# Sums of the next step's first group moved between W1 and W2 products at a step's end, on one Trainium2 core

## What is computed

```python
def step(h, _):
    agg = jax.ops.segment_sum(h[src], dst, num_segments=N) / deg
    diff = jnp.tanh(jax.nn.gelu(agg @ W1 + b1, approximate=False) @ W2 + b2)
    h = h + (diff - decay * h) * dt
    return (h, None)
...
h = jnp.maximum(_layernorm(x, axis=-1), 0.0)
x = x + _L0_gnn_ref(h, edge_index, ...)      # twelve steps
h = jnp.maximum(_layernorm(x, axis=-1), 0.0)
x = x + _L1_gnn_ref(h, edge_index, ...)      # two graph convolutions
```

## Time and profile before

| what | value |
|---|---|
| time, median of 3 runs | 1358.31 us (1358.14 to 1360.56) |
| the profiled execution: its own time | 1362.37 us |
| its span, first to last instruction | 1360.7 us |
| TensorE busy | 1276.2 us, 94% |
| VectorE busy | 392.7 us, 29% |
| ScalarE busy | 323.7 us, 24% |
| mean granted TensorE clock | 0.981 of full |

### The profile page before, as it was taken

How to read it: one execution, slowest core, us unless ns; L and a number is a source line. 1 busy time by engine, 2 the same in 40 slices (tenths; PEclk the granted TensorE clock), 3 DMA queues, 4 the chain that set the end, 5 groups by cost and what they waited for, 6 DMA issues and landing times.

```text
span 1360.7 us, 17338 instructions
## 1 busy us (share of the span) xinstructions
PE 1276.2 (94%) x7201; PEld 712.6 (52%) x7201; DVE 392.7 (29%) x792; ACT 323.7 (24%) x474; POOL 45.2 (3%) x48
## 2 busy tenths in 40 slices
PE   2875999999999999999999999999999999979998
PEld 1764356455564555545545556455554554545545
DVE  6899013113121131221311312113112131451312
ACT  1788113113121131221311312113112121330100
POOL 3900000000000000000000000000000000000000
PEclk7899999999999999999999999999999999979999
DMA  3000200000000000000000000000000001120101
GB/s 95 1 1 0 61 1 0 0 0 0 0 0 0 0 0 0 0 0 0 0 0 0 0 0 0 0 0 0 0 0 0 0 0 39 47 57 0 47 17 33
DMA packets 24541, 13.66 MB, mean 10 GB/s; under 512 B 6171, under 2 KB 23605, under 8 KB 24384
## 3 DMA queue, kind: packets, MB, share of 16 engines
q1 hardware_dynamic: 22414, 12.28, 3.5%
q10 hardware_dynamic: 1698, 0.66, 0.2%
q0 software_dynamic: 400, 0.33, 0.1%
HBM read 9.42 MB, written 3.44 MB: 9 GB/s over the span
## 4 chain that ended last, share of the span: by engine, by line
PE 86%; DVE 7%; issue 3%; ACT 2%; DMA 2%; DVEq 0%; ACTq 0%; SPq 0%; POOL 0%; POOLq 0%
PE ps L630 34%; PE ps L632 32%; PE ps L653 10%; PE ps L644 8%; DVE scratch L996 4%; ACT scratch L787 1%; PE ps L557 1%; PE ps L680 1%; DVE ps L1102 1%; DMA adj<-packed_scratch,adj 1%; ACT adj L755 1%; DMA dinv_scratch<-cols 1%; DVE lo L979 0%; DMA adj<-adj 0%; PE ps L520 0%
## 5 line engine op out<-in xcount | busy, mean ns | idle before, releaser
L630 PE MATMUL ps<-adj,hi 128*128 128x512 f16 (+2 forms) x2450 | 814.5, 353 | 9.3 <-DVE lo L979 5.8
L632 PE MATMUL ps<-adj,lo 128*128 128x512 f16 (+2 forms) x2352 | 796.2, 353 | 0.0
L630 PEld LDWEIGHTS ps<-adj,hi 128*128 128x128 f16 x2450 | 238.3, 97 | 260.2 <-issue 21.8
L632 PEld LDWEIGHTS ps<-adj,lo 128*128 128x128 f16 x2352 | 229.3, 98 | 242.9 <-issue 23.0
L1102 DVE TENSOR_TENSOR ps<-ps,bias 128x512 f32<-128x512 f32 (+1 forms) x84 | 53.8, 641 | 538.0 <-PE ps L653 538.0
L795 ACT ACTIVATE scratch<-ps 128x512 f32<-128x512 f32 (+1 forms) x84 | 46.3, 551 | 644.8 <-DVE ps L1102 644.8
L644 PE MATMUL ps<-scratch,w 128*128 128x512 f32 (+2 forms) x336 | 141.5, 544 | 18.3 <-ACT scratch L787 18.3
L787 ACT ACTIVATE scratch<-ps,b1c,cols 128x512 f32<-128x512 f32 (+2 forms) x168 | 113.4, 722 | 159.7 <-PE ps L644 158.9
L653 PEld LDWEIGHTS ps<-w,scratch 128*128 128x128 f32 x1200 | 145.0, 194 | 6.3
L653 PE MATMUL ps<-w,scratch 128*128 128x128 f32 x1200 | 147.7, 277 | 0.0
L1095 DVE TENSOR_TENSOR scratch<-ps,scratch 128x512 f32<-128x512 f32 (+2 forms) x84 | 52.0, 619 | 187.6 <-PE ps L644 132.2
(11 more groups left out here) (129 smaller groups left out, 210.1 us busy)
## 6 DMA issues: line engine op xcount, KB each, us to landing
scratch<-rdeg_scratch SPq DMA_DIRECT2D x1, 1562.5 KB
state<-in_x_dram SPq DMA_DIRECT2D x5, 256.0 KB, 4.1
scratch<-in_x_dram SPq DMA_DIRECT2D x5, 256.0 KB, 2.8
x_scratch<-state SPq DMA_DIRECT2D x5, 256.0 KB, 2.8
scratch<-dinv_scratch SPq DMA_DIRECT2D x5, 256.0 KB, 3.8
state<-x_scratch SPq DMA_DIRECT2D x5, 256.0 KB, 4.1
out_dram<-state SPq DMA_DIRECT2D x5, 256.0 KB
adj<-adj SPq DMA_DIRECT2D x1, 390.6 KB, 4.0
```

Source lines behind the costliest of these rows:

```text
L630: nc.tensor.matmul(bank, hi[:, k, :], adj[:, k, c0:c0 + n], start=(at == 0), stop=False)
L632: mm = nc.tensor.matmul(bank, lo[:, k, :], adj[:, k, c0:c0 + n], start=False, stop=(k == K_ORDER[-1][0]))
```

## The change

`edge_sums` gets a range of source tiles, and the sums of group 0 are taken in two parts. The first part (`HEAD`, eight source tiles, groups 0 and 1; in the last step `LAST_HEAD`, four tiles) is issued at the end of the step before, between `hidden(TAIL)` and `outputs(5)`. Within it the four `hi` products of source group 0 come first and then the four `lo` products. `hidden(TAIL)` writes to a bank of its own (`ps_hid_tail`, both halves in bank 7), so it no longer waits for `gelu(5)`. ScalarE and VectorE are reordered at a step's end: four `next_hi` now stand ahead of `tanh(4)` and `gelu(5)`, `next_lo(0)` ahead of `add_bias(4)`, `next_lo(1)` to `next_lo(4)` ahead of `add_bias(5)`. In the last step `norm_rows` goes from ScalarE to VectorE, as one `tensor_scalar` for each tile without the ReLU (which `norm_hi` and `lo_of` now do), `row_factors` is cut at tiles 12 and 20 and not at 12 and 16, and its parts move.

```diff
+HEAD = 2 * GROUP_TILES
+LAST_HEAD = GROUP_TILES
...
+        ps_hid_tail = [ps[:, 7, 0:P], ps[:, 7, P:2 * P]]
...
-            def edge_sums(turn, g, split, first):
+            def edge_sums(turn, g, split, first, part=(0, TILES)):
...
-                for at, (k, owner) in enumerate(K_ORDER):
+                for at in range(*part):
+                    k, owner = K_ORDER[at]
+                    if g == 0 and owner == 0:
+                        if at == 0:
+                            pe.wait_ge(his, first + 1)
+                            for i in range(GROUP_TILES):
+                                product(hi, K_ORDER[i][0], i == 0, False)
+                            pe.wait_ge(los, first + 1)
+                            for i in range(GROUP_TILES):
+                                mm = product(lo, K_ORDER[i][0], False, False)
+                        continue
...
                 def hidden(g):
...
-                    pe.wait_ge(s_gelu, t * 2 * NG + 2 * g + OPEN)
+                    pe.wait_ge(s_gelu, t * 2 * NG + (2 * g if g < TAIL else 0) + OPEN)
...
                 hidden(TAIL)
+                pe.wait_ge(s_aggT, t * NG + TAIL - 1 + OPEN)
+                if last:
+                    pe.wait_ge(s_diag, 1)
+                    edge_sums(STEPS, 0, (c_hi[0], c_lo[0]), 0, (0, LAST_HEAD))
+                else:
+                    edge_sums(t + 1, 0, (s_hi, s_lo), (t + 1) * NG, (0, HEAD))
                 outputs(TAIL - 1)
                 outputs(TAIL)
+            edge_sums(0, 0, (s_hi, s_lo), 0, (0, HEAD))
...
# VectorE, steps 1 to 11
                 means(TAIL)
+                dve.wait_ge(s_now, t + 1)
+                next_lo(0)
                 add_bias(TAIL - 2)
+                next_lo(1)
                 update(TAIL - 2)
-                dve.wait_ge(s_now, t + 1)
-                for g in range(3):
+                for g in range(2, 5):
                     next_lo(g)
                 add_bias(TAIL - 1)
                 update(TAIL - 1)
-                for g in range(3, TAIL - 1):
-                    next_lo(g)
...
# VectorE, last step
+            def norm_rows(g):
+                k0, nt = GROUPS[g]
+                dve.wait_ge(s_fac, 1 if g < 3 else 2 if g < 5 else 3)
+                dve.wait_ge(s_x2o[g], 16 * parts(g))
+                for k in range(k0, k0 + nt):
+                    last_ = V.tensor_scalar(state[:, k, :], state[:, k, :], ln_a[:, k:k + 1], ln_b[:, k:k + 1],
+                                            ALU.mult, ALU.add)
+                last_.then_inc(s_t, 1)
...
                     if g == 4:
                         row_factors(0, 12)
-                    if g == 5:
-                        row_factors(12, 16)
+                        for b in range(3):
+                            norm_rows(b)
                 means(TAIL)
-                add_loops(TAIL)
+                norm_lo(0)
                 add_bias(TAIL - 2)
+                norm_lo(1)
                 update(TAIL - 2)
-                norm_lo(0)
                 add_input(TAIL - 2)
+                row_factors(12, 20)
+                norm_rows(3)
                 add_bias(TAIL - 1)
+                norm_lo(2)
+                norm_rows(4)
                 update(TAIL - 1)
-                norm_lo(1)
-                norm_lo(2)
+                norm_lo(3)
                 add_input(TAIL - 1)
+                norm_lo(4)
                 add_bias(TAIL)
                 update(TAIL)
                 add_input(TAIL)
-                row_factors(16, TILES)
-                for g in range(3, NG):
-                    norm_lo(g)
+                row_factors(20, TILES)
+                norm_rows(5)
+                norm_rows(6)
+                add_loops(TAIL)
+                norm_lo(5)
+                norm_lo(6)
```

More of the change, by code:

```diff
@@ L611, in _, with product @@
                 pe.wait_ge(g_degk, 5 + OPEN)
-            def edge_sums(turn, g, split, first):
+            def edge_sums(turn, g, split, first, part=(0, TILES)):
                 c0, n = SPANS[g]
                 bank = ps_agg[2 if g == TAIL else g % 2][:, 0:n]
-                for at, (k, owner) in enumerate(K_ORDER):
+                his, los = split
+                def product(values, k, is_first, is_last):
+                    return nc.tensor.matmul(bank, values[:, k, :], adj[:, k, c0:c0 + n], start=is_first, stop=is_last)
+                for at in range(*part):
[9 more added lines that the diff above has]
+                        continue
                     if g == 0:
-                        pe.wait_ge(split, first + owner + 1)
+                        pe.wait_ge(los, first + owner + 1)
                         if k == SHORT:
@@ L637, in _, with step @@
             pe.wait_ge(s_w, 16 * 8)
-            def step(t):
+            def step(t, last):
                 def hidden(g):
@@ L799, in next_hi @@
                     split_hi(g, (t + 1) * NG + g + 1, next_scale[:, :])
-                def norm_rows(g, batch_):
-                    k0, nt = GROUPS[g]
-                    act.wait_ge(s_fac, batch_)
-                    act.wait_ge(s_x2o[g], 16 * parts(g))
-                    for k in range(k0, k0 + nt):
-                        last_ = nc.scalar.activation(state[:, k, :], state[:, k, :], ACT.Relu,
-                                                     bias=ln_b[:, k:k + 1], scale=ln_a[:, k:k + 1])
-                    last_.then_inc(s_t, 1)
                 def norm_hi(g):
                     act.wait_ge(s_t, g + 1)
-                    nc.scalar.activation(tiles_of(hi, g), tiles_of(state, g), ACT.Copy).then_inc(c_hi[0], 1)
+                    nc.scalar.activation(tiles_of(hi, g), tiles_of(state, g), ACT.Relu).then_inc(c_hi[0], 1)
                 act.wait_ge(s_now, t + 1)
-                for g in range(1, NG):
-                    if last and g == TAIL:
-                        norm_rows(3, 2)
-                        act.wait_ge(s_agg, (t + 1) * NG)
-                        norm_hi(0)
+                for g in range(1, TAIL):
                     if g >= 2:
@@ L822, in step @@
                     gelu(g - 1)
-                    if last and g == 4:
-                        for b in range(3):
-                            norm_rows(b, 1)
+                act.wait_ge(s_agg, (t + 1) * NG)
                 if last:
-                    norm_hi(1)
+                    for g in range(3):
+                        norm_hi(g)
+                    tanh(TAIL - 2)
+                    gelu(TAIL - 1)
                     gelu(TAIL)
-                    norm_hi(2)
+                    norm_hi(3)
                     tanh(TAIL - 1)
-                    norm_hi(3)
+                    norm_hi(4)
                     tanh(TAIL)
-                    for g in range(4, NG):
-                        norm_rows(g, 3)
-                        norm_hi(g)
-                else:
+                    norm_hi(5)
+                    norm_hi(6)
+                else:
+                    for g in range(4):
+                        next_hi(g)
+                    tanh(TAIL - 2)
+                    gelu(TAIL - 1)
                     gelu(TAIL)
-                    act.wait_ge(s_agg, (t + 1) * NG)
-                    for g in range(3):
-                        next_hi(g)
+                    next_hi(4)
                     tanh(TAIL - 1)
-                    for g in range(3, TAIL - 1):
-                        next_hi(g)
                     tanh(TAIL)
```

36 lines of the change are left out of this document (21 added, 15 removed).

## The result

The changed kernel takes 1339.44 us (median of 4 runs, 1338.63 to 1339.75) and the kernel before, run beside it, 1358.66 (1358.14 to 1360.56): a ratio of 0.9855, with a 95% interval of 0.9838 to 0.9872. The profiled execution took 1339.52 us, its span is 1337.8.

The account below looks back on a forecast made before the run. TensorE, busy 94% of the span, was taken as the bound, with VectorE setting the last step's end. Gains of 16.5 us (loop) and 3.9 us (last step), 20.4 us, gave a median of 1337.9 us, range 1334.5 to 1343.

Parts of the forecast that it names:

- The loop: End of the eleven looped steps: TensorE's wait for `gelu` goes, 1.5 us a step, 16.5 us in all (15.4 to 17.6).
- The margin at `lo(5)`: Looped steps, source group 5: `lo(5)` ends near 235.1, TensorE arrives at 236.3, so 1.2 us margin and no new wait.
- the wait moves: Rival, looped steps: `lo(5)` late by 0.8 us makes a wait at source group 5, 1347 us; chance 0.06.
- slower: Rival, looped steps: `add_bias(5)` queues behind `lo(2)` to `lo(4)`, `lo(5)` comes 3.7 us late, 1365 us; chance 0.03.
- The cover of the head: Looped step's end: reordered ScalarE and VectorE make `hi(0)`, `lo(0)`, `lo(1)` before the head wants them, least margin 2 us.
- The last step: Last step, where VectorE sets the end: last wait ends at 1214.5 with nine products left, winning 3.9 us (0.9 to 5.9).
- A scaled row: Last step, VectorE: one 128-column `tensor_scalar` costs about 0.17 us (0.13 to 0.40), with 13 rows on the chain.
- The rule on `tensor_scalar`: Scaled rows: fp32 `tensor_scalar` runs at twice `tensor_tensor` rate; if SBUF operands prevent it, 0.23 us a row, 0.8 more.
- The sum: Whole kernel: 16.5 us in the loop plus 3.9 in the last step, 20.4 us, for a median of 1337.9 us.
- It does nothing: Rival, looped steps: the 1.25 us is a wait for `hidden(5)`'s own data, so 1355 to 1358 us; chance 0.03.
- The steps win, the last step does not: Rival: only the loop's 16.5 us is won, the last step's VectorE chain needing 4 us more; 1341.8 to 1344; chance 0.12.
- The last step wins more by a clock that recovers sooner: Rival, last step: clock stays at 2.4 GHz or recovers sooner, 3 us more if TensorE does not fall, 1335; chance 0.06.

Follow-up runs that it names:

- the old banks: Changed kernel without the bank of its own for `hidden(TAIL)`, moved sums issued ahead of it: 1340.71 us, ratio 0.9850 to the kernel before.
- the second pair: Kernel before and changed kernel, each profiled and timed again with no edit: 1359.09 us and 1339.73 us.
- the rows with constants: Changed kernel with last-step rows scaled by constants 1 and 0 instead of scale and bias from SBUF: 1337.18 us, ratio 0.9831.

## Why the prediction was right, point by point

The median is 1339.44 us, forecast was 1337.9 in a range of 1334.5 to 1343. The mechanism came out as forecast. Inside the sum one term was sized too low, and one was right in part by luck.

**The loop: 16.5 us forecast, 17.7 in the traces.** The place, the cause and the order of all instructions were as forecast. The term was sized at 1.5 us a step and is 1.607 (1.600 with the old banks) in every kernel that has the head and no new wait. That lies just above the upper bound of 1.6 (17.6 us). The working gave 1.55, and I took 1.5 because the short `hidden` of before needed 0.54 us and not 0.43. That was only its start behind a wait: with both `hidden` in one block it takes the 0.43. The rest, 0.06, is rounding in my rate for `outputs`: 0.1115 us an instruction, not 0.115.

**The margin at `lo(5)`: 1.2 us forecast, 1.1 measured** from the timeline, and confirmed by the head of twelve tiles, which overruns it by 0.69 us where 0.6 was expected. This was the place on which the rivals "the wait moves" and "slower" stood. They did not come about, but they are real: too long a head gives the first in small.

**The cover of the head: right, and it was the riskiest part of the change.** The order of ScalarE and VectorE that the prediction counted as preparation is what makes the head pay; without it the kernel is 25 us slower than before.

**The last step: 3.9 us forecast, 3.8 over the two pairs of traces, and in part by luck.** A scaled row was taken as 0.17 us and is 0.26, because of two operands from SBUF; 13 of them are 1.1 us of the chain, and the last wait ended 21.98 us behind `hidden(5)` where 21.1 was forecast. That leaves 3.0 us, and it is what the second pair has (29.1 - 26.0 = 3.1), whose stretches at half clock, 5.1 and 5.5 us, are about the same, as forecast. In the first pair the stretch did not last the 6 us taken over from before but 2.7, and the tail won 4.6. The mean of the two pairs comes to the forecast by these two errors, which cancel. The four waits forecast as 1.8, 0.3, 1.0 and 5 us were 1.85, 0.39, 0.80 and 5.45.

**The rule on `tensor_scalar`.** The Trainium skill, "VectorE: DVE Perf Modes", section "The perf-mode tier table", has the fp32 `tensor_scalar` in SBUF at twice the rate of a `tensor_tensor`. The trace of the rows with constants agrees: 221 ns, where a `tensor_tensor` of 128 fp32 columns takes 292:

```profile
L1299 DVE TENSOR_TENSOR state<-state,scratch 128x128 f32<-128x128 f32 x1 | 0.3, 292 | 0.0
```

The difference is 0.55 ns a column; both durations have a fixed part, so they are not in the proportion of the rates. The sum was short all the same, since the operands are a cost beside the rate. That cost could be read before: the row of 625 columns has one operand from SBUF itself and took 0.87 ns a column all the same, and `update`, which reads one, takes 0.75 us where L1167, which reads none, takes 0.69.

**The sum.** The mean spans of the two traces of each kernel are 20.7 us apart: 17.7 in the loop, 3.5 behind the last `hidden(5)`, and 0.5 us lost ahead of the loop. Medians: 19.2 us, and 19.9 with the changed kernel run again, where 20.4 was forecast. The 0.8 to 1.5 us between traces and medians are not explained. The time ahead of the loop varies, in kernels with the same code there, between 219.1 and 225.0 us for the first `hidden(5)`; with two traces of each kernel an offset of 1 to 2 us can't be told from this.

**The rivals.** "It does nothing" falls with every trace. "The steps win, the last step does not" falls with the tails of 25.5 and 26.0 against 30.1 and 29.1. "The last step wins more by a clock that recovers sooner" came about in the first profile alone.

## What to carry to other kernels

When an in-order engine waits for a short chain on other engines, first look for work of its own whose operands are ready, and put it there; a second buffer only lets the engine run up to the next dependent instruction. Such a head pays only if its operands are made early enough by the other engines, and it delays all that stands behind it, so nothing is gained by making it longer than the wait it covers: four tiles did what eight did, and twelve cost 7.9 us. Then look again: the same move, made once more at the largest remaining wait, gave another 11 us here.
